# Second layer all in groups of seven products: the first four groups start on the first half of tokens, and three short matmuls are added to the start

## The reference

```
cond(x):  gate = x Wg^T + 0.5*(x A^T) B^T     up likewise     (width 1376, lora of rank 16, one of 16 for each sequence)
          down = (silu(gate)*up) Wd^T + lora
ffn(c):   nx = c * rsqrt(mean(c^2) + 1e-5) * ln_w
          out = (silu(nx Wg^T) * (nx Wu^T)) Wd^T             (width 1792)
result    x + ffn(cond(x))
```

## Time and profile before

| | |
|---|---|
| time, median of 3 runs | 402.79 us (402.6 to 404.47) |
| profiled execution, its own time | 402.25 us |
| its span | 400.5 us |
| TensorE busy | 395.1 us, 99% of the span |
| VectorE busy | 307.1 us, 77% |
| ScalarE busy | 235.4 us, 59% |
| granted clock of TensorE | full in all 40 slices |

### The profile page before, as it was taken

The page is one execution under the profiler, slowest core; times in us unless marked ns, Lnnn a source line. Parts: engine busy times, 40 slices in busy tenths (PEclk is TensorE's granted clock), DMA queues, the critical chain, the costliest instruction groups (busy, mean ns, idle before and its releaser), DMA issues.

```text
span 400.5 us, 5698 instructions
## 1 busy us (share of the span) xinstructions
PE 395.1 (99%) x1989; PEld 330.1 (82%) x1989; DVE 307.1 (77%) x466; ACT 235.4 (59%) x376; POOL 10.6 (3%) x13
## 2 busy tenths in 40 slices
PE   8999999999999999999999999999999999999996
PEld 6898878888888888888888888888888888888885
DVE  4799978685835547673699897878787869799993
ACT  4789786757574359822646656564646494384730
POOL 6300000000000000000000000000000000000000
PEclk9999999999999999999999999999999999999999
DMA  7630253311112630300101122313131216105112
GB/s 250 213 116 2 80 130 94 112 52 54 52 54 53 164 102 0 106 0 0 54 0 52 55 63 97 95 62 106 52 108 52 71 74 195 55 2 197 53 52 106
DMA packets 14542, 32.42 MB, mean 81 GB/s; under 512 B 2354, under 2 KB 4658, under 8 KB 14514
## 3 DMA queue, kind: packets, MB, share of 16 engines
q1 hardware_dynamic: 13936, 30.48, 24.2%
q10 hardware_dynamic: 578, 1.57, 1.0%
HBM read 29.95 MB, written 2.10 MB: 80 GB/s over the span
## 4 chain that ended last, share of the span: by engine, by line
PE 97%; DMA 1%; issue 0%; DVE 0%; DVEq 0%; SPq 0%
PE bank L1291 48%; PE bank L1592 17%; PE bank L1482 14%; PE bank L1400 5%; PE bank L1428 3%; PE bank L1447 3%; PE bank L1436 3%; PE bank L1301 2%; PE bank L1504 1%; PE bank L1496 1%; DMA wraw<-w_in 1%; PE bank L1511 0%; DVE act L920 0%; DVEq L49 0%; SPq L286 0%
## 5 line engine op out<-in xcount | busy, mean ns | idle before, releaser
L1291 PE MATMUL bank<-xs,ws 128*128 128x512 f32 x840 | 194.2, 390 | 0.0
L1291 PEld LDWEIGHTS bank<-xs,ws 128*128 128x128 f32 x840 | 156.6, 188 | 32.3 <-ACT bank L395 0.4
L395 ACT ACTIVATE xs<-act 128x512 fp32r<-128x512 f32 x71 | 42.9, 624 | 21.8 <-DVE act L985 7.6
L1482 PE MATMUL bank<-xs,wdc 128*128 128x512 f32 x240 | 55.7, 390 | 0.0
L1482 PEld LDWEIGHTS bank<-xs,wdc 128*128 128x128 f32 x240 | 44.8, 188 | 9.4 <-issue 0.2
L838 DVE TENSOR_TENSOR xs<-act,xs 128x512 fp32r<-128x512 f32 x71 | 47.5, 684 | 3.3 <-ACT xs L395 2.8
L838 DVE TENSOR_TENSOR ws<-wraw,ws 128x256 fp32r<-128x256 f32 (+2 forms) x49 | 32.4, 669 | 14.5 <-ACT ws L395 14.3
L395 ACT ACTIVATE bank<-bank 128x512 f32<-128x512 f32 x30 | 17.4, 581 | 39.8 <-PE bank L1291 38.9
L1592 PE MATMUL bank<-xs,vs 128*128 128x512 f32 x168 | 38.2, 389 | 0.0
L1592 PEld LDWEIGHTS bank<-xs,vs 128*128 128x128 f32 x168 | 31.5, 188 | 6.5
L395 ACT ACTIVATE ws<-wraw 128x256 fp32r<-128x256 f32 (+2 forms) x47 | 28.6, 619 | 11.7 <-PE bank L1291 4.1
(11 more groups left out here) (122 smaller groups left out, 419.5 us busy)
## 6 DMA issues: line engine op xcount, KB each, us to landing
wraw<-wgu_in SPq DMA_DIRECT2D x22, 512.0 KB, 3.3
wdr<-vs_in SPq DMA_DIRECT2D x7, 512.0 KB, 3.5
wraw<-vj_in SPq DMA_DIRECT2D x3, 896.0 KB, 4.6
wdr<-wd_in SPq DMA_DIRECT2D x10, 256.0 KB, 2.7
xa<-xT_in SPq DMA_DIRECT2D x4, 256.0 KB, 4.5
wraw<-w_in SPq DMA_DIRECT2D x4, 256.0 KB, 4.7
xa<-xT_in ACTq DMA_DIRECT2D x2, 512.0 KB, 6.1
bgu_raw<-bgu_in SPq DMA_DIRECT2D x32, 32.0 KB, 1.8
```

The lines of the kernel that those rows point to most:

```text
L395: return nc.scalar.activation(out_ap, in_ap, ACT.Copy, scale=scale)
L1291: ins = mm(z[:, :], ws[:, j % 2, w, s, k * P:(k + 1) * P], xs[:, c, r, k, :], start=(start and k == 0 and s == 0 and r == 0), stop=(k == 1 ...
L1482: ins = mm(z[:, :], wd[:, s, h * P:(h + 1) * P], x[r], start=(start and s == 0 and r == 0), stop=False, skip_group_check=True)
```

## The change

The eight unit products are gone. The tiles that they made become two more groups: S2 is 22, so there are 14 groups in the second layer. The first four groups (S1 to S1+3, here 0 to 3) are treated apart:

- `q1` and `q2` of all four groups (X11 and X21 only, so first half of tokens only) run first. The sums of squares of half 1 stand behind the first two `q1`.
- Then, for groups 0 and 1 together: both `p3`, both `g_prod`, both `p6`, both `p7`. Their g goes to the A bank, and `c12` adds copy and bank in two steps.
- Then groups 2 and 3 without `q1` and `q2`; group 2 also does the `p4` of group 0 and of group 1. Their q1 is saved from its bank to the buffer `sqr` (`save`) and copied from there to the B bank (`ca`).
- The weights of groups 2 and 3 get a buffer of their own, `wx`, on the front part of `wdc`; they are made while the down projection of the first layer still runs. Those of groups 0 and 1 are made earlier, between the columns of the down weights, with their sums. The last down weights (`w10`) move from `ws` to memory of their own.
- X12 alone is no longer made. Half 1 is scaled in the order 6, 7, 4, 5.
- `vs` is filled in the order 4, 5, 0, 1, 2, 3, 6.
- Three more matmuls on ones, of 256 columns each, stand behind the nine.

```
-S1, S2 = G1 - 2, G1 + NF - 4
+S1, S2 = G1 - 2, G2 - 2
-WARM = 9
+WARM, WARM_HALF = 9, 3
+V_ORDER = (4, 5, 0, 1, 2, 3, 6)
...
+        def w_slot(g):
+            return (wx if g in (S1 + 2, S1 + 3) else ws)[:, g % 2]
+        def w_next(g):
+            return {S1 + 2: S1 + 4, S1 + 3: S2}.get(g, g + 1)
+        def a_bank(g):
+            return (bank[7], bank[3])[g % 2] if g in (S1 + 2, S1 + 3) else A_BANK[g % 2]
+        def g_bank(g):
+            return A_BANK[g % 2] if g in (S1, S1 + 1) else G_BANK[g % 2]
...
 @block.scalar, from the norm of half 1
             square_hi()
+            ca(S1)
             rsqrt(1)
+            ca(S1 + 1)
             nc.scalar.preload_act_table(ACT.Silu)
-            unit_silu(4)
+            c11(S1)
+            save(S1 + 2)
             a.wait_ge(s_nx, 6)
-            hi_x(1, X12, nx1[:, 0:2, :])
-            a.wait_ge(s_nx, 8)
             hi_x(1, X22, nx1[:, 2:4, :])
-            unit_silu(5)
-            for i in range(2):
-                a.wait_ge(s_xsum[1], i + 1)
-                hi_x(1, T_SLOT[i], xsum_f[:, i])
-            hi_a(G1 + 2)
-            hi_b(G1 + 2)
+            save(S1 + 3)
+            a.wait_ge(s_xsum[1], 1)
+            hi_x(1, T_SLOT[0], xsum_f[:, 0])
+            c11(S1 + 2)
+            a.wait_ge(s_xsum[1], 2)
+            hi_x(1, T_SLOT[1], xsum_f[:, 1])
+            cm(S1)
+            cm(S1 + 1)
             a.wait_ge(s_xsum[1], 3)
             hi_x(1, T_SLOT[2], xsum_f[:, 2])
-            unit_silu(6)
-            unit_silu(7)
+            cu(S1)
             a.wait_ge(s_xsum[1], 4)
-            a.wait_ge(s_uu, 8)
-            hi_x(1, XT4, xsum_f[:, 3])
-            for j in range(S1, S2):
+            hi_x(1, T_SLOT[3], xsum_f[:, 3])
+            cu(S1 + 1)
+            c12(S1)
+            c22(S1)
+            c21(S1)
+            for j in range(S1 + 2, S2):
                 group(j, S2)
...
 @block.vector, from the end of the norm of half 1
-            for m in range(4, 8):
+            for m in (6, 7, 4, 5):
                 scale(m)
-            lo_x(1, XF["12"], xs[:, X12, 1], nx1[:, 0:2, :], xs[:, X12, 0])
+            v.wait_ge(s_nx, 8)
+            x_sum(1, 0)
             lo_x(1, XF["22"], xs[:, X22, 1], nx1[:, 2:4, :], xs[:, X22, 0])
...
+            lo_t(1, 0)
+            x_sum(1, 1)
+            c11(S1 + 1)
+            x_sum(1, 2)
+            lo_t(1, 1)
+            lo_t(1, 2)
             x_sum(1, 3)
+            c12(S1)
+            lo_t(1, 3)
+            c22_sum(S1)
+            c12(S1 + 1)
+            c11(S1 + 3)
+            for j in range(S1 + 2, S2):
                 group(j, S1, S2)
...
 @block.tensor
+            for i in range(WARM_HALF):
+                mm(B_BANK[i % 2][:, 0:256].rearrange("p (k n) -> p k n", k=2), ones[:, :],
+                   ones[:, :].unsqueeze(1).to_broadcast([P, 2, P]), start=True, stop=True)
...
-            conv(UNIT_BANK[4][0], G1, 0, 0, range(3))
+            q1(S1)
+            q1(S1 + 1)
             sum_squares(1, 0)
             sum_squares(1, 1)
-            conv(UNIT_BANK[4][0], G1, 0, 0, range(3, KT)).then_inc(s_ug, 1)
-            conv(UNIT_BANK[4][1], G1 + 1, 0, 0).then_inc(s_uu, 1)
-            conv(UNIT_BANK[5][0], G1, 1, 0).then_inc(s_ug, 1)
-            pe.wait_ge(s_ev, 8)
-            conv(UNIT_BANK[5][1], G1 + 1, 1, 0).then_inc(s_uu, 1)
-            pe.wait_ge(s_xlo[1], XF["12"])
-            pe.wait_ge(s_var, 2)
-            for g in range(2):
-                for n in range(6, 8):
-                    conv(UNIT_BANK[n][g], G1 + g, n - 6, 1).then_inc((s_ug, s_uu)[g], 1)
-            for j in range(S1, S2):
-                group(j, S1)
+            q2(S1)
+            q2(S1 + 1)
+            q1(S1 + 2)
+            q1(S1 + 3)
+            q2(S1 + 2)
+            q2(S1 + 3)
+            for j in range(S1, S1 + 2):
+                p3(j)
+            for j in range(S1, S1 + 2):
+                g_prod(j)
+            for j in range(S1, S1 + 2):
+                p6(j)
+            for j in range(S1, S1 + 2):
+                p7(j)
+            for j in range(S1 + 2, S2):
+                group(j)
```

More of the change, by code:

```diff
@@ L732, in group @@
                     cm(j)
-                if j + 1 < last:
-                    hi_a(w_of(j + 1))
+                if w_next(j) < last:
+                    hi_a(w_of(w_next(j)))
                 cu(j)
[L736 to L740, removed]
+                if w_next(j) < last:
+                    hi_b(w_of(w_next(j)))
+                if S1 + 2 < j < S2 - 1 and j % 2 == 1:
+                    hi_v((j - S1) // 2 - 1)
+                if j % 2 == 0 and j != S1 + 2:
                     c11(j)
@@ L757, in _ @@
                     cl(S1 - 1)
+                elif n in (5, 7):
+                    hi_a(G1 + (n - 5) // 2)
+                elif n in (6, 8):
+                    hi_b(G1 + (n - 6) // 2)
             for t in range(2):
@@ L784, in _ @@
             hi_x(1, X21, nx0[:, 2:4, :])
+            for j in range(G1 + 2, G1 + 4):
+                hi_a(j)
+                hi_b(j)
             keep_y(4)
@@ L1135, in group @@
                         c22_act(j - 1)
[L1136 to L1141, removed]
+                if w_next(j) < last:
+                    sums(w_of(w_next(j)))
+                if j > S1 + 2 and j % 2 == 0:
+                    lo_v((j - S1) // 2 - 2)
+                elif j > S1 + 2:
+                    sums_v((j - S1) // 2 - 1)
                 if j > first and j % 2 == 0:
                     c21(j - 1)
-                if j + 1 < last:
-                    lo_a(w_of(j + 1))
+                if w_next(j) < last:
+                    lo_a(w_of(w_next(j)))
                     if j == 0:
                         x_sum(0, 3)
-                    lo_b(w_of(j + 1))
+                    lo_b(w_of(w_next(j)))
                 if j == 0:
@@ L1178, in _ @@
                 lo_ac(n)
+                if n in (5, 7):
+                    sums(G1 + (n - 5) // 2)
+                    lo_a(G1 + (n - 5) // 2)
+                elif n in (6, 8):
+                    lo_b(G1 + (n - 6) // 2)
             for i in range(4):
@@ L1204, in _ @@
             lo_x(1, XF["21"], xs[:, X21, 1], nx0[:, 2:4, :], xs[:, X21, 0])
+            lo_a(G1 + 2)
+            lo_b(G1 + 2)
+            sums(G1 + 3)
+            lo_a(G1 + 3)
+            lo_b(G1 + 3)
             first_square()
@@ L1310, in q1 @@
                 pe.wait_ge(s_walo, w_of(j) - 1)
-                if j >= 2:
+                if j >= 2 and j not in (S1 + 2, S1 + 3):
                     pe.wait_ge(s_c11[j % 2], j // 2)
@@ L1349, in q2 @@
             def q2(j):
-                pe.wait_ge(s_ca, j + 1)
-                ins = product(A_BANK[j % 2], j, W12, X21, False)
+                if j in (S1 + 2, S1 + 3):
+                    pe.wait_ge(s_save, j - S1 - 1)
+                else:
+                    pe.wait_ge(s_ca, j + 1)
+                ins = product(a_bank(j), j, W12, X21, False)
                 if j >= S1:
@@ L1373, in p7, with group @@
                 product(B_BANK[j % 2], j, WS3, XT3, False).then_inc(s_p7, 1)
-            def group(j, first):
-                q1(j)
+            def group(j):
+                if j not in (S1 + 2, S1 + 3):
+                    q1(j)
                 g_prod(j)
@@ L1381, in group @@
                 else:
-                    if j > first:
+                    if j == S1 + 2:
+                        p4(S1)
+                    if j > 0:
                         p4(j - 1)
                     p6(j)
-                q2(j)
+                if j not in (S1 + 2, S1 + 3):
+                    q2(j)
                 p3(j)
```

196 lines of the change are left out of this document (88 added, 108 removed).

## The result

The changed kernel takes 404.3 us (median of 22 runs, 403.85 to 404.91), the kernel before 402.85 us in the same comparison (22 runs). The ratio is 1.003, with a 95% interval of 1.002 to 1.004. 404.0 us and a change of less than 0.5% were forecast. The 12 matmuls are gone, and the kernel is still 1.45 us longer.

What follows compares the result with a forecast made beforehand. Taken as bound by its matmuls, TensorE being busy for 99% of the span: -2.72 saved + 4.08 of waits + 0 = +1.36 us, 403.61 against the profiled execution, 404.15 against the median; forecast 404.0, range 401.4 to 405.5.

Steps and rivals of the forecast that it cites:

- What is free: Weights of groups 0 to 3, `wx` and SyncE's queue: the new work there fits and costs nothing.
- rival D: New weights do not fit before `keep_y(4)` (0.4 us of room): up to some 1.5 us more, 405.5; chance 0.10.
- 1, q2 of group 1: Hand-over to half 1: q2 waits 0.06 us for copy `ca(S1+1)`, which stands behind `rsqrt`.
- 2, first p3: After the norm: p3 waits 0.48 us, as the first sum stands ahead of the low part of X22.
- 3, p7 of group 0: p7 waits 0.33 us for XT3, whose high part ScalarE makes only after both `cm` copies.
- 4, p7 of group 1: p7 waits 1.28 us, the largest, for `cu(S1+1)`, queued on ScalarE behind the fourth sum's high part.
- 5, p4 of group 1: p4 waits 0.60 us for `c22_sum(S1+1)`, behind other steps, `c12(S1+1)` among them, on VectorE.
- 6, p4 of group 2: p4 waits 0.79 us for `c22_sum(S1+2)`, behind group 4's weights, `nt1` and `c12`.
- The three short matmuls: At the kernel's start, before the first real matmul: cost 0, at worst 0.7 us; sparing late-clock executions counted as nothing.
- A: Hand-over between halves: the waits do not come, only the saving of 2.72 us, so 400.1 us; chance 0.12.
- B: Half of the waits, those from VectorE's backlog being least certain: 2.3 us against 2.72, so 402.4, no change; chance 0.15.
- Rival C: The clock falls between the six waits in 36 us; 9 slower matmuls cost 2.0 us more, 406; chance 0.08.

Runs made afterwards that it cites:

- e3: The changed kernel with the high part of the third sum moved ahead of the two `cm` copies on ScalarE: 402.6 us.
- e11: The changed kernel with `c22_sum` of group 1 between `c12`'s additions and multiplication, that of group 2 before `nt1` and `c12`, on VectorE: 403.08 us.
- e7: The changed kernel with third sum before `cm`, `c22_sum` of groups 1 and 2 early (wrong output), and squares of half 1 behind 9 matmuls: 400.88 us.
- e6: The changed kernel with third sum before `cm` and `c22_sum` of groups 1 and 2 early (wrong output, for times alone): 401.35 us.
- e8: The changed kernel with three moves: third sum before `cm`, `c22_sum` of groups 1 and 2 earlier (output kept right), squares behind 9 matmuls: 400.62 us.
- X22 first: The changed kernel with the low part of X22 moved before the first sum on VectorE: 404.37 us.
- e1: The changed kernel without the three short matmuls on ones: 404.66 us.

## Why the prediction was right, step by step

The saving of 12 matmuls was sized rightly; the three moves show 2.06 of its 2.72 us. *What is free*: the new weights ended at 189.04 by the trace (forecast 188.7), `keep_y(4)` started at 189.18, and the first product at 193.20, so rival D did not happen, with little to spare: VectorE's next step came 0.77 us after the weights, `keep_y(4)` 0.14 us.

The steps, each with the wait forecast and the bracket after:

| step | forecast | bracket | lost, start to start |
|---|---|---|---|
| 1, q2 of group 1 | 0.06 | none | 0.21 |
| 2, first p3 | 0.48 | 0.52 | 0.74 |
| 3, p7 of group 0 | 0.33 | 0.27 | 0.53 |
| 4, p7 of group 1 | 1.28 | 1.01 | 1.26 + 0.13 |
| 5, p4 of group 1 | 0.60 | 0.34 | 0.51 + 0.15 |
| 6, p4 of group 2 | 0.79 | 0.61 | 0.80 + 0.13 |
| sum | 3.54, with 0.54 for longer first matmuls 4.08 | 2.75 | 4.46 |

The right column is the next start less the start before it and 0.2267 us for each matmul between; the second number is what the six matmuls after the wait took over 1.36. With 0.06 around the sums of squares TensorE lost 4.51 in all, 4.31 more than before, so the term of 4.08 was 0.23 too small.

The error lies in the first three steps. With 0.09 for each first matmul they were forecast at 1.14 us and lost 1.48; steps 4 to 6 were forecast at 2.94 and lost 2.98. Three prices were off:

- The first matmuls after a wait cost 0.13 to 0.15, and not 0.09 as the four short ones of the earlier trace rows had it.
- The first sum started at 203.49, not at 203.15. `rsqrt` is 0.13 of that. The rest is in the norm: by the earlier trace rows the next step came 202.79 - 196.50 = 6.29 us after `rsqrt`, which gives 203.25 and not 203.15, and the first sum, which needs all scalings, came 6.40 us after it.
- The hand-over to TensorE was taken as 0.04 throughout, but after a low part of 1024 columns it is 0.14 to 0.15 (XT3: 214.55, p7 at 214.69). This VectorE row, the low part of X22, ends at 205.85, and p3 starts at 206.00:

```profile
204.63 1.22 DVE L861 TENSOR_TENSOR xs<-nx,xs 128x1024 fp32r<-128x1024 f32 x1
```

The five waits with a bracket are at the place and with the releaser that was named, and each was removed by its own order (e3: 3 and 4; e11: 5 and 6; e7 against e6: 2). `rsqrt` came at 197.09, 0.59 later than in the earlier trace rows and not 0.46. The forecast called itself wrong if the waits after 193 came to less than 2.7 us and did not say how they are counted: the brackets sum to 2.75, just above that mark, while the loss from start to start is 4.51, and this is what the time follows. It also took 2.0 us for about what can't be told from no change; 22 runs each did tell 1.45 (1.002 to 1.004).

The three short matmuls: 0.06 us later at the first real one (5.89 against 5.83), so 0 at the median was right. Left open in the forecast was whether they spare the executions in which the clock rises late. Mostly they do; this lowers the mean by some 0.6 us in each of the three pairs, the median by 0.25 to 0.36.

Of the rivals, A (only the saving comes) and B (half the waits) are refuted by the profile, and e8 shows what A needed. Rival C, the clock falling between the waits, is refuted: the 24 matmuls from 223.54 take 5.63 us, the pace of 0.2267, and five gaps of up to 1.0 us within 25 us did not cost the clock. The Trainium skill's advice against gaps between bursts (TensorE: Matmul & The Clock Gate, "Why this matters for your kernels"), on which the prediction leaned for this rival, is meant for longer gaps than these, and the trace agrees with it.

## What to carry to other kernels

When an engine is busy for 99% of the span, a change that removes work from it is worth its saving less every wait it brings, so write the new order down place by place for all in-order queues, with durations from the trace; here that gave the sign and the size, while busy shares would have given 2.7 us of gain. A copy that waits for TensorE must not stand in a queue ahead of work that is ready and on the path; moving one operation ahead of two such copies won 1.7 us. And take out a wait only together with what is behind it: "X22 first" removed one and made another of the same size.

## What was not expected

The times of the kernel before fall into two clusters 1.7 us apart, and three matmuls of 256 columns on ones, put where TensorE idles 0.49 us, all but remove the upper one (2 of 106 runs against 13 of 35). The granted clock in the profile's row reads full in every slice even for the execution in which the first real matmuls ran at the lower level (e1); only their durations show it.
